# Attention groups: the next group's first score unit is issued ahead of the turn of this group's row maxima

## What is computed

```
q = (layernorm(x) @ Wq)   as 16 heads of 16 channels
k, v = ctx @ Wk, ctx @ Wv as 16 heads of 16 channels
scores = q @ k.T / sqrt(16)          # 256 x 256 for each batch and head
layer 0: scores = -inf above the diagonal and where the mask is set
attn = softmax(scores)               # along the keys
x = x + (attn @ v, heads joined) @ Wout + b_out
```

## Time and profile before

| | us |
|---|---|
| three runs | 1469.08, 1475.82, 1478.23; median 1475.82 |
| the profiled execution, its own time | 1471.67 |
| span of the profiled execution | 1470.0 |
| attention 0, from its first score to its last matmul | about 52.9 to 290 |
| attention 1, from its first score on | 667.7 to about 895 |
| TensorE busy in the whole span | 1165.3 (79%) |
| VectorE, ScalarE, GpSimd busy | 719.9, 585.0, 402.2 |

### The profile page before, as it was taken

The page is one execution under the profiler, slowest core; times in us unless marked ns, Lnnn a source line. Parts: engine busy times, 40 slices in busy tenths (PEclk is TensorE's granted clock), DMA queues, the critical chain, the costliest instruction groups (busy, mean ns, idle before and its releaser), DMA issues. The chain is left out here.

```text
span 1470.0 us, 26772 instructions
## 1 busy us (share of the span) xinstructions
PE 1165.3 (79%) x8532; PEld 1009.6 (69%) x8532; DVE 719.9 (49%) x1623; ACT 585.0 (40%) x1184; POOL 402.2 (27%) x601
## 2 busy tenths in 40 slices
PE   4689986765359999626565875699999999999997
PEld 3466764554358888513333544699999999999997
DVE  6545544444212222267444675555555555555556
ACT  1355653411112322115454672244444444444432
POOL 5267662013501111263556301260000000000062
PEclk8699998857779999857888897599999999999999
DMA  6645766004479999543344332112233223223132
GB/s 164 112 114 139 164 145 191 1 1 127 144 298 327 329 326 332 188 110 67 76 94 85 54 55 93 58 63 73 65 107 96 80 90 95 86 85 96 52 87 87
DMA packets 94170, 182.26 MB, mean 124 GB/s; under 512 B 15843, under 2 KB 64413, under 8 KB 87824
## 3 DMA queue, kind: packets, MB, share of 16 engines
q1 hardware_dynamic: 81776, 141.40, 35.6%
q0 software_dynamic: 12320, 39.94, 7.8%
HBM read 134.29 MB, written 47.72 MB: 124 GB/s over the span
## 5 line engine op out<-in xcount | busy, mean ns | idle before, releaser
L1972 PE MATMUL e_ps<-xT_e,wp_e 128*128 128x384 f32 (+1 forms) x1344 | 245.0, 331 | 4.8 <-DVE wp_e L1846 4.8
L699 DVE TENSOR_REDUCE att_ps<-att_ps 128x2 f32<-128x512 f32 (+1 forms) x224 | 154.9, 697 | 185.5 <-PE att_ps L963 103.1
L1972 PEld LDWEIGHTS e_ps<-xT_e,wp_e 128*128 128x128 f32 x1344 | 221.6, 188 | 6.2 <-issue 4.9
L961 PE MATMUL att_ps<-ks,qs 96*128 96x256 bf16 (+1 forms) x512 | 109.5, 282 | 88.0 <-DMA qs<-parts 46.6
L886 ACT ACTIVATE probs<-att_ps 128x384 f32<-128x384 f32 (+1 forms) x256 | 130.5, 544 | 48.2 <-PE att_ps L993 37.3
L1902 DVE TENSOR_TENSOR hid_e<-act_a_e,e_ps 128x256 f32<-128x256 f32 (+2 forms) x176 | 87.0, 494 | 115.4 <-ACT act_a_e L1804 106.8
L1804 ACT ACTIVATE act_a_e<-e_ps 128x256 f32<-128x256 f32 (+2 forms) x176 | 77.8, 442 | 159.9 <-PE e_ps L1972 159.2
L1989 PE MATMUL e_ps<-wp_e,hidp_e 128*128 128x256 f32 (+1 forms) x1008 | 138.3, 281 | 3.0 <-DVE xres L1862 1.2
L1904 DVE TENSOR_TENSOR hidp_e<-hid_e,hidp_e 128x256 fp32r<-128x256 f32 (+2 forms) x176 | 87.7, 498 | 95.5 <-ACT hidp_e L1808 95.5
L1808 ACT ACTIVATE hidp_e<-hid_e 128x256 fp32r<-128x256 f32 (+2 forms) x176 | 83.8, 476 | 127.0 <-DVE hid_e L1902 125.3
L1989 PEld LDWEIGHTS e_ps<-wp_e,hidp_e 128*128 128x128 f32 (+1 forms) x1008 | 130.5, 183 | 5.0 <-issue 4.1
(11 more groups left out here) (216 smaller groups left out, 1980.9 us busy)
## 6 DMA issues: line engine op xcount, KB each, us to landing
w_e<-in_W SPq DMA_DIRECT2D x48, 1024.0 KB, 7.6
w_e<-in_W SPq DMA_DIRECT2D x57, 384.0 KB, 3.0
ks<-parts SPq DMA_DIRECT2D x96, 128.0 KB, 5.0
qs<-parts SPq DMA_DIRECT2D x96, 128.0 KB, 4.1
parts<-cut SPq DMA_DIRECT2D x24, 384.0 KB, 5.6
rows<-zeros POOLq DMA_DIRECT2D x8, 768.0 KB, 4.9
x_e<-rows SPq DMA_DIRECT2D x48, 128.0 KB, 6.4
done<-y_e POOLq DMA_DIRECT2D x48, 128.0 KB, 6.3
```

The lines of the kernel that those rows point to most:

```text
L699: dve.tensor_reduce(tops_at(at[3])[:, qt, x0:x0 + heads], src, AX.X, ALU.max).then_inc(reduced, 1)
L961: last = pe.matmul(out, qs[0:KS, j, hd, qt * P:(qt + 1) * P], ks[0:KS, j, hd, 0:keys(qt)], start=True, stop=not causal)
L1972: last = pe.matmul(ps[:, bank + u % 2, 0:n], weights(lot, c, pw)[:, (b * DC + d) * P:(b * DC + d + 1) * P], xT[:, px, d, t0:t0 + n], start ...
```

## The change

On TensorE, in every group, `score_next(0)` is issued ahead of `turn_tops(at)` and not behind it. Nothing is added or removed, and the four other engines' orders are the same in both kernels. The last group of each attention has no next group, so the order there is unchanged.

```
@@ -1084,8 +1084,8 @@
                         if more and u < NU:
                             score(after(at), u)
 
+                    score_next(0)
                     turn_tops(at)
-                    score_next(0)
                     if started:
                         value(prior(at))
                     score_next(1)
```

## The result

| | before | changed |
|---|---|---|
| median | 1473.16 us | 1458.46 us |
| runs | 9, from 1469.08 to 1478.51 | 9, from 1453.19 to 1464.26 |
| ratio | | 0.9912, 95% interval 0.9886 to 0.9937 |
| the profiled execution, its own time | 1471.67 us | 1463.19 us |
| its span | 1470.0 us | 1461.4 us |

That is 13 us less, between 9 and 17 by the interval. The forecast was 1471 us in a range from 1463 to 1480. It is still within 1% of the time before.

What follows compares the result with a forecast made beforehand. Waits, not a full engine, were taken to bound both attentions: stack loads in attention 0, GpSimd's rows in attention 1 until 810 us. Terms 2.6 + 1.3 + 0.8 - 1.6 = 3.1 us faster; prediction 1471 us, range 1463 to 1480.

Steps and rivals of the forecast that it cites:

- the 1.6 us charged: Attention 0, group 3: the turn queued behind the stack wait lengthens six tails, 1.6 us lost in all.
- a loss of 8.4 us: Attention 0, group 3: upper end of the moved wait's cost, 6 x 1.4 us if ScalarE's copy lay bare.
- what is saved at a turn is the smaller of the wait and the time that the unit held back `value`: Turns with a wait: in attention 1 after 810 us, eight waits save 0.32 us each, 2.6 us.
- the groups without a wait: Attention 0, where TensorE did not wait at the turn: its work in the group is unchanged in sum, zero.
- the fixed pieces: Four stretches holding no long supply wait, at the ends of attention 0 and in attention 1; 4.7 us forecast for them.
- the row path's 1.38 us: Turn, ScalarE's copy, transposed score, uncovered: 1.38 us; attention 1's new cover of 1.45 us just exceeds it, nothing charged.
- the first batch of attention 1: Forecast 0 us gained, since GpSimd was taken to set the time up to 810 us.
- the first batch of attention 0: Ahead of the first DMA leg: 0.40 us at one turn plus 0.4 at the first turn, 0.8 us saved.
- Number 2: Rival: the wait moves from the turn to the transposed score, leaving only the 1.6 us loss; 1473.3 to 1477.4 us, 14%.
- Number 3: Rival: longer idleness before the stacks drops TensorE's clock in tails, costing 6 us; 1474.6 to 1478.7 us, 12%.
- Number 4: Rival: GpSimd's clears fall among stack loads, 7.2 us more per DMA leg; three legs give about 1490 us, 5%.
- Number 5: Rival: all 62 moved units earn their place, 27 us, about 1445 us, faster by more than 1%; 5%.

Runs made afterwards that it cites:

- e6: Changed kernel with unit 1 moved between the turn and `value`; 1461.47 us, ratio 0.9932 to the kernel before.
- e9: The kernel before run again, unedited, for a second profile; 1474.71 us, ratio 1.0017 to the kernel before.
- e5: The changed kernel run again, unedited, for a second profile; 1464.10 us, ratio 0.9932 to the kernel before.
- e1: Changed kernel with the new order kept in attention 0 only; 1466.48 us, ratio 0.9951 to the kernel before.
- e2: Changed kernel with the new order kept in attention 1 only; 1461.02 us, ratio 0.9931 to the kernel before.
- e4: Changed kernel with the new order kept in group 3 only; 1469.29 us, ratio 0.9988 to the kernel before.
- e3: Changed kernel with the new order in groups 0 to 2 only, group 3 as before; 1462.83 us, ratio 0.9933 to the kernel before.
- e7: Changed kernel with both first units ahead of the turn; 1465.00 us, ratio 0.9955 to the kernel before.
- e8: Changed kernel plus 32 filling matmuls ahead of each stack wait in attention 0, from batch 1's units on; 1464.45 us, ratio 0.9940 to the kernel before.

## Why the forecast fell short

**What held.** Waits bound both attentions. The six stack waits stayed, and from the first batch end to the last arrival nothing that groups 0 to 2 save comes through. VectorE still waits for GpSimd in batches 1 to 4 of attention 1 (133.3 and 134.6 us before, 131.2 and 132.7 after). Over all profiles, four with this attention's order as before take 132.5 to 134.9 us there and five with the new one 131.2 to 132.8. So some 2 us may be earned there against the forecast of nothing, and no run separates them from chance. The moved wait in group 3 costs less than the 1.6 us charged: the tail grew by 0.1 to 0.2 us at equal clock. The rule that I quoted from the Trainium skill, DMA: Bandwidth & Descriptors, section Rules for kernel authors (wait late on a transfer), gave a loss of 8.4 us at this place. That did not come, since the work behind the wait was covered, as the rows had said. The DMA legs are less even than the three shown ones: the first two before are 22.7 us (81.64 to 104.37) and 22.5 (112.86 to 135.38), where I had 21.1 to 21.4.

**The step that failed: "what is saved at a turn is the smaller of the wait and the time that the unit held back `value`", 0.32 us in eight places, and the groups without a wait "zero".** From batch 5 on attention 1 earned 3.2 us in the place of 2.6, and all the fixed pieces some 6.5 us by the order in the place of 4.7. The filled wait by itself was even worth less than 0.32 us a turn (0.22 in e6: 4.80 to 4.58, 4.98 to 4.76). Two things beside it were missed.

1. *The pair.* The turn writes 8 partitions in the last column tile, and the first three matmuls of `value` use the other three. Next to each other they start together or 0.10 us apart. The turn's own cost falls from 0.21 to 0.10 us, and the switch from the turn to a full-width unit and back to `value` is gone. e6 moves unit 1 between them and shows it: 0.15 us a turn in the waiting groups of attention 1. With it such a turn earned 0.37 to 0.38 (4.80 to 4.43, 4.98 to 4.60). It also paid in a group of attention 0 in which TensorE never waited, where the distance of 5.05 us became 4.89, and in batch 7 it paid nothing. I had costed full groups at zero. It was to be read beforehand, in the last group, which has no unit. These two rows of the trace before stand beside the turns at 277.72 and 277.77:

```profile
277.73 0.42 PE L1007 MATMUL att_ps<-probs,v 128*32 128x256 f32 x3
277.83 0.81 PE L1007 MATMUL att_ps<-probs,v 128*32 128x256 f32 x13
```

I took the row path's 1.38 us from there and did not look at where `value` starts beside the turn. The Trainium skill, TensorEngine Tiling (Array Packing), section Tiling Modes, says that different tiles can run in parallel and that changing the mode drains the engine. The trace agrees with the first part, with starts 0.00 to 0.01 us apart. How much of the 0.15 us is the drain no run here separates.

2. *The places.* Of the eleven distances from batch 5 on ten became shorter, and not eight: some without a wait before also did, as 5.20 to 5.03 and 5.39 to 5.02. The step from group 3 into the next batch earned 0.5 us twice (5.49 to 4.98, 5.11 to 4.61). That piece gained 3.2 and 3.9 us against 2.6; the second holds the 1.3 us group of e9 and the 0.6 us stack wait of e5, and without them it is 3.2 too.

**Costed at zero: the first batch of attention 1.** I let GpSimd set the time up to 810 us. But in batch 0 GpSimd is itself waiting. Before and after:

```profile
684.75 0.22 POOL L507 TENSOR_SCALAR spread<-mean_var 128x2 f32<-128x2 f32 x1 [20.75 <-DVE mean_var L692]
```

```profile
682.54 0.22 POOL L507 TENSOR_SCALAR spread<-mean_var 128x2 f32<-128x2 f32 x1 [20.23 <-DVE mean_var L692]
```

It waits over 20 us for VectorE, which in turn waits for TensorE's scores. The batch took 1.2 and 1.7 us less. In e1 the same batch took 20.43 us with this attention's order as before, so not all of it is the order. The second step of the batch, from the turn of group 1 to that of group 2, shows the rest. Here it is before, after, in e1 (order as before) and in e2 (new order):

```profile
677.82:683.88 6.06, 5.61 (x40) 2.85 (x40) 3.73 (x9) 3.95 (x7) 0.00 (x0) 0.80 0.01 1
676.47:681.68 5.21, 4.96 (x42) 3.27 (x41) 3.74 (x9) 3.95 (x7) 0.00 (x0) 0.86 0.00 1
674.21:679.20 4.99, 4.55 (x40) 2.67 (x41) 3.73 (x9) 3.95 (x7) 0.00 (x0) 1.00 0.06 7
673.20:677.87 4.67, 4.34 (x41) 2.78 (x40) 3.73 (x9) 3.95 (x7) 0.00 (x0) 1.00 0.03 3
```

With this step at 1.00 in both, the batch takes 20.43 us by the old order and 19.70 by the new, and 0.7 us is the order's part. The rest is the clock of the one step.

**Under-sized: the first batch of attention 0**, 3.0 us against 0.8. In two ordinary groups the distance fell from 5.05 to 4.89 and from 5.52 to 4.90, together 0.8 us. From group 3's turn to the batch's end it fell from 6.02 to 5.56, since the unit no longer stands between them; e4 has this part alone (24.11 against 24.56). In sum that is 1.2 us. The first group fell by 1.8 us (1.5 against e9), and that is the clock. Windows of this group before and after:

```profile
57.10:65.00 7.90, 7.89 (x46) 5.99 (x46) 2.43 (x5) 3.19 (x6) 0.53 (x1) 0.66 0.80 137
```

```profile
57.50:63.70 6.20, 5.63 (x47) 4.38 (x47) 2.28 (x5) 3.36 (x6) 0.90 (x2) 1.00 0.77 128
```

TensorE sat idle 1.30 us ahead of this turn before, and 0.54 after, with the unit in the gap. From this turn to the next the clock stood at 0.66 before and at 1.00 after. Over all fourteen profiles it stood at 1.00 in three of the eight with a unit in the gap (the changed kernel twice, and e3), and in none of the six without. In the other five it stood at 0.67 to 0.72: e1, with the same order, took 7.88 us, no less than e9's 7.70. In the three the unit's last matmul ahead of the turn already takes 0.22 us and not 0.31, so the clock had risen before the turn:

```profile
56.52 0.31 PE L963 MATMUL att_ps<-shut,identb 128*128 128x128 bf16 x1
...
56.73 0.22 PE L963 MATMUL att_ps<-shut,identb 128*128 128x128 bf16 x1
```

In the old order TensorE is idle at this point. That the new order makes the earlier rise possible fits these rows and is not shown; the 1.6 us in the mean of the two pairs are luck as far as the forecast goes.

**The rivals.** Number 2 did not happen: TensorE's work between turn and transposed score came to 1.38 us, just the row path; e7 shows how near it is. Number 3, the clock, came true in part in the profiles. The tails sum to 40.3 and 37.5 us, where the kernel before has 35.9 and 33.2, and e8 shows that it is the clock. The moved turn, which the rival blamed, does not do it by itself (e4, 33.4). It was outweighed, and the timed runs don't resolve it. The Trainium skill, TensorE: Matmul & The Clock Gate, section HAM oscillation, has a burst after a DMA wait start throttled. Behind three of the four waits of 3.49 to 5.12 us in the changed kernel the trace agrees (0.66 to 0.68). Behind the fourth, 3.57 us, it shows 0.77, and behind waits of about 2 us 0.77 or 1.00 for the same kind of work. Number 4 did not come; the last leg took 25.7 us. Number 5 was written off because only waits were thought to earn; the pair earns in some full groups too, but its 27 us did not come.

**What stays open.** Of the 9.3 us of the fixed pieces the order has about 6.5: 1.2 and 1.4 at the ends of attention 0, 0.7 and 3.2 at the ends of attention 1. The clock has the rest. With the possible 2 us of batches 1 to 4 that makes 7 to 9 us, against timed gains of 13 (9 to 17) and 10 us (6 to 14). The spans of the two pairs of profiles differ by 5.8 us in the mean, and by the pieces all of it lies in attention 1. What attention 0 gains at its ends is lost among its legs and tails (161.5 to 176.6 us over these profiles), and that a trace of a single execution can't settle. So the failed step explains about 2 of the 7 to 10 us by which the forecast fell short, and the overcharged wait 1 us; the rest stays open. The gain of e1 and e2 in timed runs, 7 and 10 us, has the same reserve.

## What to carry to other kernels

Before costing a move by the wait that it fills, look at what becomes neighbours. In this kernel a small matmul next to others in different column tiles cost half of what it cost next to a full-width one, and this paid in some groups without a wait as well. If one place in the trace already has the new order (here the last group), take the whole distance from it and explain each tenth that differs. For an engine "that sets the time", check in each stretch whether it isn't itself waiting.

## What the runs showed of the hardware

- A turn of two 8-partition matmuls costs 0.21 us ahead of a full-width unit and 0.10 us ahead of `value`. Where TensorE came to the turn without a wait, the first three matmuls of `value` start within 0.01 us of it.
- The same code in the same place ran at a granted clock of 0.63 to 0.72 or of 1.00: the first group of attention 0 took 7.6 to 8.4 or 6.21 us. Behind an idle gap of 1.30 us it was never at 1.00 (six profiles), behind gaps of 0.44 to 0.59 us three times in seven.
- Thirty-two filling matmuls ahead of a wait for DMA changed the tails behind it: nine of ten ran at 1.00 (5.8 to 6.0 us) in one profile of either kernel, and without the filling six of twenty in two profiles of either (the slowest 8.5 us at 0.66). In the timed runs it had no effect.
